# Tile 1's transposes behind tile 0's up products, and eight second-weight loads that ask for the last residual alone

## The reference

```python
x = x + _L0_xattn_ref(_layernorm(x, axis=-1), ctx_1024, ctx_1024, ...)
x = x + _L0_ffn_ref(_layernorm(x, axis=-1), ...)
x = x + _L1_xattn_ref(_layernorm(x, axis=-1), ctx_1024, ctx_1024, ...)
x = x + _L1_ffn_ref(_layernorm(x, axis=-1), ...)
```

```python
h = x @ W_in + b_in
t = h.reshape(B * S, -1)
logits = t @ W_gate + b_gate
probs = jax.nn.softmax(logits, axis=-1)
topv, topi = jax.lax.top_k(probs, TOP_K)                    # 2 of 8 experts
topv = topv / jnp.sum(topv, axis=-1, keepdims=True)
route = jnp.zeros_like(probs).at[jnp.arange(t.shape[0])[:, None], topi].set(topv)
mid = jax.nn.relu(jnp.einsum('nd,edh->neh', t, W1) + b1)    # 256 -> 1024, "up"
eout = jnp.einsum('neh,ehd->ned', mid, W2) + b2             # 1024 -> 256, "down"
moe_out = jnp.einsum('ne,ned->nd', route, eout)
out = moe_out.reshape(B, S, -1) @ W_out + b_out
```

## Time and profile before

| what | value |
|---|---|
| median of 3 runs | 1117.26 us (1112.96 to 1118.88) |
| profiled execution | 1113.62 us, of which the span is 1111.5 us |
| PE busy | 938.6 us (84%) |
| DVE busy | 755.5 us (68%) |
| ACT busy | 479.9 us (43%) |
| POOL busy | 279.9 us (25%) |
| DMA | 98.66 MB, mean 89 GB/s |
| chain that ended last | PE 49%, DVE 32%, ACT 6%, DMA 5%, issue 4% |

### The profile page before, as it was taken

The page is one execution under the profiler, slowest core; times in us unless marked ns, Lnnn a source line. Parts: engine busy times, 40 slices in busy tenths (PEclk is TensorE's granted clock), DMA queues, the critical chain, the costliest instruction groups (busy, mean ns, idle before and its releaser), DMA issues.

```text
span 1111.5 us, 20311 instructions
## 1 busy us (share of the span) xinstructions
PE 938.6 (84%) x6717; PEld 571.9 (51%) x6717; DVE 755.5 (68%) x1945; ACT 479.9 (43%) x1056; POOL 279.9 (25%) x246
## 2 busy tenths in 40 slices
PE   6969796886986999999998776888988898876785
PEld 3636554654653777888874532233333343345564
DVE  6483969688698766666663376785678857554666
ACT  4354553343423444444442312445666667532222
POOL 1333817141303144443321001100010011113453
PEclk9989998997988999999999986786999997788998
DMA  9441020005239111111118564523073045242231
GB/s 298 160 164 77 1 77 1 20 22 150 57 118 300 47 50 50 50 45 55 49 31 212 102 170 61 96 31 68 2 125 67 3 109 144 90 152 82 85 99 34
DMA packets 70385, 98.66 MB, mean 89 GB/s; under 512 B 8812, under 2 KB 57199, under 8 KB 67984
## 3 DMA queue, kind: packets, MB, share of 16 engines
q1 hardware_dynamic: 60144, 61.67, 20.6%
q0 software_dynamic: 10144, 35.69, 11.8%
HBM read 71.04 MB, written 27.15 MB: 88 GB/s over the span
## 4 chain that ended last, share of the span: by engine, by line
PE 49%; DVE 32%; ACT 6%; DMA 5%; issue 4%; another core or an unknown queue 2%; POOL 1%; SPq 0%; ACTq 0%; DVEq 0%; POOLq 0%
PE pb L1044 9%; PE pb L1064 7%; DVE MX L2030 5%; PE pb L1154 4%; PE pb L1065 3%; PE pb L844 3%; PE pb L831 3%; PE pb L808 2%; PE pb L1178 2%; PE pb L1132 2%; PE pb L877 2%; PE pb L887 2%; ACT EX L1472 2%; DVE w L1728 2%
## 5 line engine op out<-in xcount | busy, mean ns | idle before, releaser
L1410 ACT ACTIVATE m<-pb,b1m 128x128 f32<-128x128 f32 x404 | 115.1, 369 | 173.2 <-PE pb L1044 148.5
L2030 DVE TENSOR_REDUCE MX<-pb 128x1 f32<-128x512 f32 x256 | 158.5, 683 | 41.9 <-PE pb L1132 41.6
L1472 ACT ACTIVATE EX<-pb 128x512 f32<-128x512 f32 x256 | 137.1, 598 | 114.8 <-PE pb L1178 113.8
L1064 PE MATMUL pb<-w,mh 128*128 x404 | 149.5, 379 | 13.5 <-DVE ml L1930 11.6
L1044 PE MATMUL pb<-xt,w1h 128*128 128x128 f16 x1616 | 157.1, 221 | 2.8 <-issue 2.8
L1044 PEld LDWEIGHTS pb<-xt,w1h 128*128 x1616 | 120.6, 99 | 40.4 <-issue 4.8
L1044 PE MATMUL pb<-xt,w1l 128*128 128x128 f16 x808 | 113.3, 221 | 2.4 <-issue 2.4
L1065 PE MATMUL pb<-w,ml 128*128 x404 | 110.1, 273 | 0.0
L802 PE MATMUL pb<-identh 128*128 128x512 f16 x370 | 92.6, 403 | 14.7 <-DVE identh L1581 6.9
L1132 PE MATMUL pb<-KS,QS 48*128 48x512 f32 x256 | 69.0, 525 | 22.1 <-DVE MX L2030 13.4
L1178 PE MATMUL pb<-QS,KS 49*128 49x512 f32 x256 | 77.0, 507 | 8.9 <-ACT EX L1472 6.9
(11 more groups left out here) (324 smaller groups left out, 1631.2 us busy)
## 6 DMA issues: line engine op xcount, KB each, us to landing
SR<-in_w1m SPq DMA_DIRECT2D x20, 512.0 KB, 5.0
SR<-in_w2m SPq DMA_DIRECT2D x13, 512.0 KB, 4.8
KS<-kd SPq DMA_DIRECT2D x48, 128.0 KB, 5.3
QS<-qd POOLq DMA_DIRECT2D x18, 256.0 KB, 9.9
kd<-KHL POOLq DMA_DIRECT2D x8, 512.0 KB, 5.7
vd<-VAB POOLq DMA_DIRECT2D x4, 1024.0 KB, 4.4
rows<-HL POOLq DMA_DIRECT2D x8, 512.0 KB, 4.2
GB<-outs SPq DMA_DIRECT2D x8, 512.0 KB, 7.3
```

Source lines behind the costliest of these rows:

```text
L1064: pe.matmul(k.ap, h, M.w2[hc][:, bass.ds(regs[j] * 4, 2 * D)], start=hc == 0, stop=False)
L1410: ins = act.activation(M.m32[x % 2][:, h4, :], k.ap[:, h4 * TOK:(h4 + 1) * TOK], M.func, bias=M.b1[:, bass.ds(reg + 4 * g + h4, 1)], scale ...
L1472: act.activation(EX[m % len(EX)][:, i, :], k.ap, ACT.Exp, scale=0.25).then_inc(k.out, 1)
L2030: v.tensor_reduce(mx[:, t, 2 * s + j:2 * s + j + 1], k.ap, AX.X, ALU.max).then_inc(k.out, 1)
```

## The change

In stream "p" the order of loads and the buffers are changed. Load 1 took the buffer `SR2`, which waits for a split of stream "m"; that buffer now belongs to load 12 alone. Loads 1 to 8 wait for the last residual only. Load 9 lies in the place of chunk 11 and waits for the split of "m" that load 1 waited for. One more staging buffer is placed where chunk 6 will be written, so chunk 6 itself comes at load 6. The waits of ACT and of SP are moved to match.

In the first mixture PE does `load(1)` after `up(0)` and not before it, with three fillers ahead of `up(0)`, and DVE copies tile 1's rows between the two middle values of tile 0. The second mixture keeps its order: there the count of fillers is 0, and both loads stay ahead.

```diff
-P_ORDER = 4, 5, 6, 3, 0, 1, 2, 7, 8, 9, 10, 11, 12, 13, 14, 15
-P_SLOTS = "p0", "p1", "p2", "p3", "p4", "p5", "w1", "w2", "w3", "w4", "w0", "w5"
+P_ORDER = 4, 5, 3, 0, 1, 2, 6, 7, 8, 9, 10, 11, 12, 13, 14, 15
+P_SLOTS = "p0", "p1", "p2", "p3", "p4", "p5", "p6", "w1", "w3", "w4", "p7", "w2", "w5"
...
-        SRD = [... for i in range(7, 12)]
+        SRD = [... for i in range(6, 12)]
...
-  p=(..., SRW + SR + SRD, [4, 5, 0, 1, 2, 6, 7, 8, 9, 10, 3, 4, 5, 0, 11, 2]),
+  p=(..., SRW + SR + SRD, [4, 0, 1, 2, 6, 7, 8, 9, 10, 11, 3, 4, 5, 0, 12, 2]),
...
   # SP, fetch(i)
-                    if tag == "p" and i < 2:
-                        w.wait_ge(*lo_token("m", 12 + i))
-                    if tag == "p" and i == 2:
+                    if tag == "p" and i == 0:
+                        w.wait_ge(*lo_token("m", 12))
+                    if tag == "p" and i == 1:
                         w.wait_ge(sem("x1"), NB)
                     if tag == "p" and i == 9:
+                        w.wait_ge(*lo_token("m", 13))
+                    if tag == "p" and i == 10:
                         w.wait_ge(*lo_token("m", 15))
...
   # SP, experts
-                    for half, i in ((1, 3), (0, 13)):
+                    for half, i in ((1, 2), (0, 13)):
...
   # PE, experts: up(0), the first loads, and the loop
                     if j == 0:
                         w.wait_ge(*lo_token("mn"[L]))
+                        fill(eU, (3, 0)[L])
...
-                kx = {j: load(j) for j in range(2)}
+                kx = {j: load(j) for j in range((1, 2)[L])}
...
+                    if L == 0 and j == 0:
+                        kx[1] = load(1)
                     if j + 2 < M.n:
                         kx[j + 2] = load(j + 2)
...
   # ACT, split
-                    if tag == "p" and i == 3:
+                    if tag == "p" and i == 2:
                         w.wait_ge(*lo_token("m", 14))
-                    if tag == "p" and i >= 7:
-                        w.wait_ge(*lo_token("p", i - 2 if i < 15 else 12))
+                    if tag == "p" and i >= 6:
+                        w.wait_ge(*lo_token("p", i - 2))
...
   # DVE, experts
                 load(0)
-                load(1)
+                if L:
+                    load(1)
...
                 if L == 0:
-                    up(0, gs)
+                    up(0, gs[:1])
+                    load(1)
+                    up(0, gs[1:])
```

More of the change, by code:

```diff
@@ L245, in build @@
         SRW = [nc.alloc_sbuf_tensor_at(f"SRW{i}", [128, CH], F32, offset=WA.start + 4 * i * K) for i in range(3)]
-        SRD = [nc.alloc_sbuf_tensor_at(f"SRD{i}", [128, CH], F32, offset=MZ.start + (64 + 4 * i) * K) for i in range(7, 12)]
+        SRD = [nc.alloc_sbuf_tensor_at(f"SRD{i}", [128, CH], F32, offset=MZ.start + (64 + 4 * i) * K) for i in range(6, 12)]
         SRD.append(nc.alloc_sbuf_tensor_at("SRD12", [128, CH], F32, offset=FZ.start + 12 * K))
@@ L423, in build @@
                       m=(blocks(E0.w1h, E0.w1l, a["w1m0"]), SR + SRS, turn(8, 3) + [3, 4, 5, 0, 1, 2, 5, 0]),
-                      p=([blocks(E0.w2h, E0.w2l, a["w2m0"])[i] for i in P_ORDER], SRW + SR + SRD, [4, 5, 0, 1, 2, 6, 7, 8, 9, 10, 3, 4, 5, 0, 11, 2]),
+                      p=([blocks(E0.w2h, E0.w2l, a["w2m0"])[i] for i in P_ORDER], SRW + SR + SRD, [4, 0, 1, 2, 6, 7, 8, 9, 10, 11, 3, 4, 5, 0, 12, 2]),
                       n=(blocks(E1.w1h, E1.w1l, a["w1m1"]), SR1, [2, 3, 4, 5, 0, 1, 2, 3]), o=(back_first(blocks(E1.w2h, E1.w2l, a["w2m1"])), SR2, [0, 1, 0, 1, 2, 3, 0, 1]))
```

## The result

| what | before | after |
|---|---|---|
| median of 20 runs each | 1117.87 us (1107.88 to 1124.69) | 1110.17 us (1101.07 to 1118.58) |
| ratio | | 0.9934, 95% interval 0.9907 to 0.9961 |
| profiled execution, its span | 1113.62, 1111.5 us | 1111.1, 1108.8 us |
| PE, DVE, ACT, POOL busy | 84, 68, 43, 25% | 85, 68, 43, 25% |
| chain | PE 49%, DVE 32%, DMA 5% | PE 51%, DVE 32%, DMA 4% |

The changed kernel is faster by 7.4 us (0.66% of 1117.87); the interval is 4.4 to 10.4 us. I had forecast 1113.5 us, a gain of 3.6 us. The measured median lies inside the range, but its gain is twice the forecast one.

A forecast was written before the change was run, and what follows sets the result against it. Waits for load 1 and tile 1's rows were taken to bound the kernel up to PE's mixture. DVE's 0.55 + 4.15 - 0.46 = 4.24 us, with PE's clock, became 3.6 us: forecast 1113.5 us, range 1108.8 to 1118.2.

The forecast's parts named there:

- What bounds: Up to tile 0's last down product at 375.80: two DMA waits, load 1 (4.33 us) and tile 1's rows (6.86 us).
- The loads, 0.55 us: Routing block: split 1 loses its 1.74 us wait, but PE's projections let only 0.55 us reach the fourth addition.
- Split 9, 4.15 us: On DVE: split 9 follows tile 0's copy (ended 358.20) instead of tile 1's (362.35), 4.15 us earlier.
- Tile 1's copy between the middle values, 0.46 us: On DVE: tile 1's copy now stands ahead of split 12 and costs 0.42 us plus 0.04 to start.
- PE as the next limit: PE from tile 1's up products to tile 0's last down product: gain 4.2 us at full clock, 2.9 at half.
- PE is idle before it for some 3 us: Ahead of tile 1's up products: PE idles some 3 us, so 3.5 us at half rate may add 1.75 us.
- the middle, 3.6 us: Gain taken between 4.2 us (full clock) and 2.9 us (half clock), as the trace could not tell which.
- The first wait whole: Rival in the routing block: all 1.74 us of load 1's wait come back, gain 5.4 us, 1111.8 us; chance 0.12.
- Tile 1's rows late: Rival: tile 1's rows hold DVE's copy, gain only 0.5 to 2.5 us, near 1115.7 us; chance 0.20.
- Half clock to the end: Rival: tile 1's up and tile 0's down products all at half clock, 2.5 us later, 1119.8 us; chance 0.06.
- The change does nothing: Rival: the transposes move but DVE's splits bind elsewhere, gain under 0.6 us, 1117 us; chance 0.05.
- I put the gain on the median: Whole time: the 3.6 us gain taken off the runs' median of 1117.26 us, giving 1113.7, taken as 1113.5.

The follow-up runs named there:

- the loads alone: Kernel before with only the changed load order, PE's and DVE's order as before: 1115.69 us against 1115.44, ratio 0.9986, stretch 48.43 us (48.60 before).
- the experts' part alone: Kernel before with only tile 1's transposes and copy moved and the three fillers added, loads as before: 1111.01 us, ratio 0.9955, stretch 44.98 us.
- the late rows: Changed kernel with the gathers of tiles 1 and 2 exchanged, so tile 1's is issued third: one execution 1088.63 us, stretch 44.09 us.
- 76 fillers: Changed kernel with 76, not 64, filler products ahead of the last routing block's transposes, run twice: ratios 0.9950 and 0.9945, stretch 42.83 and 42.84 us.

## Why the prediction was right, and where not

**What bounds.** Right. DVE's splits 9 and later hung on tile 1's rows and no longer do; the whole stretch moved with them, and PE's mixture followed.

**The loads, 0.55 us.** The way was right: the third and fourth projection limit what comes back, and of split 1's 1.74 us only 0.81 reached the fourth addition, 0.74 tile 0's copy. The term was mis-sized by 0.26 at that addition: I let the fourth projection start where the third's record ends (338.41) and take its 1.13 us, but records of products in a row overlap, and 16 took 5.67 us where 12 had taken 4.80, 0.87 more. I had charged nothing for the loads' traffic beside the gather. In the changed kernel PE waited only 0.19 us for tile 1's rows, off DVE's path, but with the loads alone 0.37 us went there. I had not seen that this term is worth 0.17 without the second part.

**Split 9, 4.15 us.** Measured 4.89 - 0.74 = 4.15: exact, since after the change split 9 stands 0.61 us behind tile 0's copy, as it stood behind tile 1's.

**Tile 1's copy between the middle values, 0.46 us.** It cost 0.34 (4.89 - 4.55). Split 15 then waited 1.24 us for ACT in place of 1.19. The sum for DVE was 4.24; measured 4.50.

**PE as the next limit.** Both cases came. In two of three executions PE ran tile 1's up products at full clock and DVE and PE met: split 15 ended at 369.65 + 1.23 = 370.88 and the last down product started at 371.01. Forecast was full 4.2 or half 2.9; measured 4.50 and 2.75. The step in front of them was wrong: "PE is idle before it for some 3 us". PE waited 0.19 and 0.62 us there in the first execution, 1.55 in the second and 0.94 in the third. In the new order PE has tile 0's up products there, 3.37 of 3.60 us busy, and in the first and third execution the half clock fell under these, where ACT's high half 12 comes last and hides it (359.88 and then the activations at 360.84, for before):

```profile
359.88 1.06 ACT L1365 ACTIVATE w<-SR 128x1024 f16<-128x1024 f32 x1 [0.20 <-DVE w L1733]
360.84 1.12 ACT L1415 ACTIVATE m<-pb,b1m 128x128 f32<-128x128 f32 x4
```

It lay there too for the experts' part alone, without the three fillers and with the late rows, so in five of the six executions of this order with 64 fillers. So the middle, 3.6 us, was too low for most executions by 0.9: 0.6 for taking the middle and not the full clock's 4.2, and 0.3 in the terms above. Why the half clock falls where it does the runs do not show: with 76 fillers PE waited 1.56 and 1.53 us at the same place, and the clock stayed full. The Trainium skill, page "TensorE: Matmul & The Clock Gate", section "What's actually happening", says that the point of a change of clock does not hang on when the kernel starts and so differs from run to run. The trace agrees that it differs: the same code had its half clock at 30.6 to 34.0 us after the first transposes in one execution and at 38.3 to 41.7 in another. The page's advice against idle time, in the section "Why this matters for your kernels", held ahead of the routing block (0.06 of 2.90 us busy, then 0.50). With 76 fillers the clock fell although PE had been idle for no more than 0.74 us at a time since the fillers began.

**Rivals.** The first wait whole (gain 5.4): no, the projections held. Tile 1's rows late: no, they had slack even with their gather moved back by one. Half clock to the end: no, 0.50 ended by 361.3 in the first profile (the window from there shows 1.00), by 366 in the second. The change does nothing: no.

**The whole time.** The step that failed is "I put the gain on the median" with the gain of this stretch alone. 1113.5 was too high by 3.3 us. Of this 0.9 are the terms above (0.6 the clock's, 0.3 DVE's), and the rest is not explained. That the median still lay in the range was luck: its lower edge was 1108.8 and not 1111.8 only because I had moved it by 3 us for the runs' spread, and no term of the sum gave 7.4 us. The chance of 0.17 for over 0.5% came from that spread too.

## What to carry to other kernels

Ask of every in-order engine what stands behind a wait, and not only how long the wait is: moving four transposes behind work that was ready freed three splits on another engine, 4.15 us of a 4.28 us hole. A gain that ends at a DMA is worth only what the DMA lets through: the loads' 0.65 us at the gather's list left 0.17 where split 9 stood behind that gather, and 0.55 where it did not. And where half clock may fall on either side of a hidden stretch, forecast two cases with a chance each, not their middle.

## What the runs showed of the hardware

- The same program has its half clock at different places in different executions: under tile 0's up products in two of the changed kernel's three profiles, under tile 1's in the third, with stretches 1.75 us apart.
- With 76 fillers the granted clock fell from 0.99 to 0.50 right behind a window in which PE was busy 2.00 of 2.00 us, mostly with 8-column single-precision products. The idle times ahead of that window were 0.28 and 0.74 us.
- The wait for a gather of 128 rows was 5.39 and not 6.86 us when one load of 0.5 MB beside it was sent earlier (one execution).
- A conversion of 128 x 8 values to integers (`ri`, on the chain) took 1.72 us on DVE in the last routing block, and 0.17 us in the block before it. In the last block POOL's subtraction `HL` (2.12 us) runs beside it, and both end within 0.03 us of each other. Whether the one holds up the other no run tested. From the kernel before, DVE and then POOL:

```profile
342.17 1.72 DVE L1834 CAST ri<-rank 128x8 int32<-128x8 f32 x1
```

```profile
341.74 2.12 POOL L2224 TENSOR_TENSOR HL<-XN,HL 128x1024 f16<-128x1024 f32 x1 [34.37 <-ACT HL L1378]
```

- One kernel's level moved by 1.5% between jobs (medians 1100.76 and 1117.33), more than twice the effect of this change: only runs of one job tell such a change.
